# Maximum product ahead of the score product, and maximum ahead of the band, in the steps of a cross attention

## What is computed

```
Q = (query @ Wq + bq).reshape(Bsz, S, NUM_HEADS, D_K)
K = (key @ Wk + bk).reshape(Bsz, S, NUM_HEADS, D_K)
V = (value @ Wv + bv).reshape(Bsz, S, NUM_HEADS, D_K)
scores = jnp.einsum('bqhd,bkhd->bhqk', Q, K) / math.sqrt(D_K)
...
scores = scores + bias[None]
scores = jnp.where(key_padding_mask[:, None, None, :], -jnp.inf, scores)
attn = jax.nn.softmax(scores, axis=-1)
out = jnp.einsum('bhqk,bkhd->bqhd', attn, V).reshape(Bsz, S, D_MODEL)
return out @ Wo + bo
```

## Time and profile before

| | |
|---|---|
| median of 3 runs | 2393.33 us (2389.95 to 2396.13) |
| profiled execution | 2390.08 us, span 2388.2 us |
| mean granted clock of TensorE | 0.958 of full |
| busy: PE, DVE, ACT, POOL | 2129.7, 1505.1, 1178.9, 1364.8 us |
| first pass, its units | about 94 to 883 us |

### The profile page before, as it was taken

The page is one execution under the profiler, slowest core; times in us unless marked ns, Lnnn a source line. Parts: engine busy times, 40 slices in busy tenths (PEclk is TensorE's granted clock), DMA queues, the critical chain, the costliest instruction groups (busy, mean ns, idle before and its releaser), DMA issues. The chain is left out here.

```text
span 2388.2 us, 43597 instructions
## 1 busy us (share of the span) xinstructions
PE 2129.7 (89%) x12672; PEld 972.8 (41%) x12673; DVE 1505.1 (63%) x4218; ACT 1178.9 (49%) x2316; POOL 1364.8 (57%) x1452
## 2 busy tenths in 40 slices
PE   3899999999999963899999999999985787899997
PEld 1333333333333311344444444444433343455554
DVE  3788888888888843566566566565534577344443
ACT  3355555555555442355545455454445474455554
POOL 3267767677677670265656555655651565455554
PEclk7999999999999986899999999999997898999999
DMA  5413323232232203544534345253403675666665
GB/s 173 151 58 105 101 84 116 70 109 94 89 107 76 84 6 131 146 122 118 150 95 142 117 132 143 88 152 98 142 32 134 125 163 117 109 117 115 111 110 88
DMA packets 222851, 263.78 MB, mean 110 GB/s; under 512 B 39192, under 2 KB 165004, under 8 KB 222388
## 3 DMA queue, kind: packets, MB, share of 16 engines
q1 hardware_dynamic: 197612, 212.79, 29.6%
q0 software_dynamic: 22976, 48.38, 11.7%
q10 hardware_dynamic: 2072, 0.28, 0.1%
HBM read 162.12 MB, written 86.80 MB: 104 GB/s over the span
## 5 line engine op out<-in xcount | busy, mean ns | idle before, releaser
L496 ACT ACTIVATE a_pt<-a_bank 128x512 f32<-128x512 f32 x512 | 305.2, 597 | 361.1 <-DVE a_bank L603 357.7
L1382 DVE CUSTOM_DVE_ANT_0 b_bank<-b_bank,b_tri 128x256 f32<-128x256 f32 (+3 forms) x512 | 253.8, 497 | 303.0 <-PE b_bank L1519 298.2
L614 DVE CUSTOM_DVE_ANT_0 a_bank<-a_bank,a_strip 128x512 f32<-128x512 f32 x512 | 353.4, 691 | 4.9 <-PE a_bank L757 4.0
L1167 POOL TENSOR_TENSOR b_acc<-b_acc,b_pt 128x256 f32<-128x256 f32 (+2 forms) x384 | 271.3, 727 | 89.5 <-ACT b_pt L1256 72.3
L406 POOL TENSOR_TENSOR a_acc<-a_acc,a_pt 128x512 f32<-128x512 f32 x256 | 317.1, 1274 | 3.6 <-ACT a_pt L496 3.1
L603 DVE TENSOR_TENSOR a_bank<-a_bank,a_band 128x256 f32<-128x256 f32 (+1 forms) x512 | 205.9, 403 | 132.2 <-PE a_bank L744 130.9
L1256 ACT ACTIVATE b_pt<-b_bank 128x256 f32<-128x256 f32 (+2 forms) x384 | 144.0, 384 | 190.1 <-PE b_bank L1503 179.6
L744 PE MATMUL a_bank<-a_q_stack,a_k_stack 128*128 128x512 f16 x512 | 196.3, 385 | 12.2 <-ACT a_pt L496 11.8
L757 PE MATMUL a_bank<-a_k_stack,a_q_stack 97*128 97x512 f16 x512 | 196.1, 383 | 3.6 <-DVE a_low L614 3.5
L1849 POOL DMA_INDIRECT out_dram<-c_z,c_to_row x72 | 114.1, 1585 | 138.2 <-DMA out_dram<-c_z,c_to_row 101.2
L403 POOL TENSOR_TENSOR a_acc<-a_pt 128x512 f32<-128x512 f32 x128 | 160.0, 1271 | 4.3 <-ACT a_pt L496 4.3
(11 more groups left out here) (346 smaller groups left out, 5439.4 us busy)
## 6 DMA issues: line engine op xcount, KB each, us to landing
b_q_stack<-qk_rows SPq DMA_DIRECT2D x192, 128.0 KB, 2.7
a_q_stack<-qk_rows SPq DMA_DIRECT2D x96, 128.0 KB
a_k_stack<-qk_rows SPq DMA_DIRECT2D x96, 128.0 KB
b_k_stack<-qk_rows SPq DMA_DIRECT2D x96, 128.0 KB, 2.7
a_sums<-in_x SPq DMA_DIRECT2D x34, 256.0 KB, 2.9
qk_rows<-a_qk_hi SPq DMA_DIRECT2D x64, 128.0 KB, 1.7
qk_rows<-a_qk_lo SPq DMA_DIRECT2D x64, 128.0 KB, 1.8
out_dram<-a_sums SPq DMA_DIRECT2D x32, 256.0 KB, 2.0
```

Of the source, the lines that this page charges most:

```text
L496: nc.scalar.activation(pt[:, n % SLOTS, :], st_bank[n % 2][:], ACT.Exp).then_inc(exped, 1)
L614: nc.vector.tensor_tensor_reduce(out=max_bank[step % 2][:], in0=max_bank[step % 2][:], in1=strip[:, g * HG + hh, at:at + S], scale=-1.0, s ...
L1167: nc.gpsimd.tensor_tensor(sums_of, sums_of, probs(n), ALU.add).then_inc(pooled, 1)
L1382: nc.vector.tensor_tensor_reduce(out=max_bank[step % 2][:, 0:w], in0=max_bank[step % 2][:, 0:w], in1=tri[:, at:at + w], scale=-1.0, scalar ...
```

## The change

In a step, TensorE issues the maximum product first and the score product behind it, and VectorE does the reduction first and the addition behind it. All waits stay with their instructions. The diff, whole but for lines that only moved along:

```
@@ VectorE, body(kind, b, u)
                 for step in range(STEPS):
-                    n = step - L
-                    if has_unit(kind, n):
...
-                        dve.wait_ge(scored, b * UNITS + n + 1)
-                        nc.vector.tensor_tensor(st_bank[n % 2][:, c0:c1], st_bank[n % 2][:, c0:c1], band[:, h, at:at + c1 - c0],
-                                                ALU.add).then_inc(biased, 1)
                     if has_max(kind, step):
...
                                                        accum_out=low[:, g % 2, hh * NT + i:hh * NT + i + 1]).then_inc(lowered, 1)
+                    n = step - L
+                    if has_unit(kind, n):
...
+                        dve.wait_ge(scored, b * UNITS + n + 1)
+                        nc.vector.tensor_tensor(st_bank[n % 2][:, c0:c1], st_bank[n % 2][:, c0:c1], band[:, h, at:at + c1 - c0],
+                                                ALU.add).then_inc(biased, 1)
@@ TensorE, body(kind, b, u)
                 for step in range(STEPS):
+                    if has_max(kind, step):
...
+                        if kind != "first" or step >= 3 * GS + 2:
+                            pe.wait_ge(lowered, b * UNITS + step + (GS - 1))
+                        mm(max_bank[step % 2][:], q_stack[0:MASK + 1, h, i * P:(i + 1) * P], k_stack[0:MASK + 1, h, :],
+                           start=True, stop=True).then_inc(maxed, 1)
                     n = step - L
                     if has_unit(kind, n):
...
                         mm(st_bank[n % 2][:], k_stack[:, h, j * P:(j + 1) * P], q_stack[:, h, :], start=True,
                            stop=True).then_inc(scored, 1)
-                    if has_max(kind, step):
...
-                        mm(max_bank[step % 2][:], q_stack[0:MASK + 1, h, i * P:(i + 1) * P], k_stack[0:MASK + 1, h, :],
-                           start=True, stop=True).then_inc(maxed, 1)
                     fill(kind, b, step, False)
```

More of the change, by code:

```diff
@@ L617, in body @@
                                                        accum_out=low[:, g % 2, hh * NT + i:hh * NT + i + 1]).then_inc(lowered, 1)
+                    n = step - L
+                    if has_unit(kind, n):
+                        j, hh = divmod(n % GS, HG)
+                        h = n // GS % NG * HG + hh
+                        c0, c1 = max(0, j * P - BAND // 4), min(S, j * P + P + BAND // 4)
+                        at = c0 - (j * P - BAND // 4)
+                        dve.wait_ge(scored, b * UNITS + n + 1)
+                        nc.vector.tensor_tensor(st_bank[n % 2][:, c0:c1], st_bank[n % 2][:, c0:c1], band[:, h, at:at + c1 - c0],
+                                                ALU.add).then_inc(biased, 1)
                     for t, (at, _, _) in enumerate(moments_at(kind)):
@@ L731, in body @@
                 for step in range(STEPS):
+                    if has_max(kind, step):
+                        g = (step // GS + 1) % NG
+                        i, hh = divmod(step % GS, HG)
+                        h = g * HG + hh
+                        if step % GS == 0:
+                            pe.wait_ge(stacked[g], (b + (2 if g == 0 else 1)) * STK)
+                            if kind == "first":
+                                pe.wait_ge(sides_stored, 16 * 3)
+                        if kind != "first" or step >= 3 * GS + 2:
+                            pe.wait_ge(lowered, b * UNITS + step + (GS - 1))
+                        mm(max_bank[step % 2][:], q_stack[0:MASK + 1, h, i * P:(i + 1) * P], k_stack[0:MASK + 1, h, :],
+                           start=True, stop=True).then_inc(maxed, 1)
                     n = step - L
```

## The result

| | before | changed |
|---|---|---|
| median of 4 runs each, same chip | 2393.69 us (2389.95 to 2396.13) | 2424.78 us (2420.23 to 2428.61) |
| ratio | 1 | 1.0130 [1.0108, 1.0153] |
| profiled execution, span | 2390.08, 2388.2 us | 2420.23, 2418.3 us |
| first batch, from one M transpose to the next batch's | 94.66 us | 101.98 us |
| a steady batch (five of the six; the third: 101.20, 105.60) | 101.08 us | 105.26 us |

The account below looks back on a forecast made before the run. TensorE's own stream was taken to bound the first pass. Seven batches at 2.6 us plus 0.4 for the last gave 18.6 us, added to 2393.3 for 2412 us; range 2398 to 2426.

Parts of the forecast that it names:

- The mechanism: First pass: addition waits for the reduction, exponential runs 0.61 us later in VectorE's step; score product's slack shrinks by 0.39 plus 0.04.
- step 7: Steady batch: would lose 0.25 us, swallowed by the wait for a query's low half at step 8.
- (a) to (d): Steady batch, steps 12 to 14, 18 to 24, 25 to 31, and 35, 39, 47, 51: 2.6 us lost together.
- (d): Steps 35, 39, 47 and 51, no late eviction: score product's slack falls short of 0.48, 0.72 us lost.
- (a) to (c): Steps 12 to 14, 18 to 24, 25 to 31: evictions behind late exponentials delay low halves; 0.2, 1.05 and 0.66 us lost.
- Larger: Each of a batch's 16 groups of four steps loses 0.39 us: 44 us, 2437; chance 0.13.
- The clock: More short idle times bring the lower clock, one stretch per batch: 7 us on top, 2419; chance 0.05.
- No change: Slack absorbs the late exponential or evictions are ready earlier; only (d) counts: 5 us, 2398; chance 0.14.
- faster: With the maximum ahead, VectorE works through TensorE's waits at the score product: up to 12 us back, 2381; chance 0.05.

Follow-up runs that it names:

- e3: The changed kernel without the empty instruction between VectorE's wait for the maximum product and the reduction; 2420.50 us, 1.0104 of the kernel before.
- e9: The kernel before without the empty instruction ahead of the reduction; 2397.00 us, 0.9997 of the kernel before.
- e1: The kernel before with the new order on TensorE only, VectorE still adding first; 2408.17 us, 1.0042 of the kernel before.
- e4: The kernel before with one more empty instruction, between VectorE's wait for the score product and the addition; 2399.49 us, 1.0007 of the kernel before.

## Why the prediction was right, and where it was not

The time came out inside the range, and the mechanism is the one forecast; the size was 1.7 times the likeliest one.

- **What bounds the pass: right.** Only the first pass moved. It is 35.7 us longer in the profile: 7.3 for the first batch, 25.3 for the six steady ones, about 3 in the last. The other two passes took 1505.4 us before and 1499.8 after; in the profiles of this study they lie between 1500 and 1515, so that is no effect of the change.
- **The mechanism: right.** The exponential starts 1.10 us after VectorE's step does (452.39 to 453.49) and did so after 0.46 (434.20 to 434.66): 0.64 later, forecast 0.61. Losses stand at the four places named, and step 7's was in good part swallowed at steps 8 and 0. Parts (a) to (d) measured 0.4, 1.1, 0.8 and 1.4 us, and step 16 another 0.15; forecast 0.2, 1.05, 0.66 and 0.72. So the largest share of the 1.6 us a batch by which the forecast fell short is (d)'s, 0.7.
- **The step that failed** is the sentence that a step of VectorE "is as long as before and begins at the same moment, since the maximum product now stands in the score product's old slot". The slot is the same, but a reduction that was waited for starts 0.53 us behind its product, the addition 0.41 to 0.43: an empty instruction stands between wait and reduction. The slack of a score product shrank by about 0.54, not by 0.43, at every place at once: steps 35 and 51 lost 0.30 where I had 0.14 and 0.15, and step 16, which I had taken as free, began to pay. Nor is such a step always "as long as before": (d) was to be "with no late eviction", but in step 44 there is one, VectorE's step is 0.23 longer, most of it (0.19) in waiting for that eviction, and step 47 lost 0.55 where I had 0.25, with the empty instruction and, in e3 (0.51), nearly as much without. e3 measures 103.91, 2.83 over before, beside a forecast of 2.6. That the two sums are so near is partly luck: in e3, (d) is 1.06 and not 0.72, while steps 7, 8 and 0 together give 0.18 back. The 0.53 was to be had from the trace of before (90.69 and 91.24), had I looked up how long each of the two waits takes to let go.
- **The range: held by luck.** 31.1 us lies outside the 10 to 28 that had the chance of 0.63. The upper end, 2426, added 13 us for "(a) to (c) half as large again"; but these three were 7 x 1.91 = 13.4 us in all, so half of them is 6.7, and the end by its own rule would have been 2419, below the 2424.78 measured. Nor were these parts what grew most: they were larger by some 0.4 us a batch, (d) by 0.7, and the first and the last batch by 5 to 8 us together.
- **First and last batch: mis-sized.** I charged the first 2.6; it lost 5.0 to 7.7. Without output fills in steps 12 to 27 it has less to cover lateness with, part of it is the clock, and near copies of the kernel before scatter by some 3 us there without either (e9). How it divides was not tried. The last lost about 3, not 0.4; TensorE still waits there for GpSimd's sums, but these come later themselves, as they need the exponentials. That is argued from GpSimd's inputs, not shown by a run.
- **The rivals.** *Larger*, with a loss in each group: no, whole groups of four, such as steps 52 to 59, lose nothing. *The clock*: it fell in the first batch (1.7 and 3.4 us' worth), where the change is not shown to be what brings it, and not where I had put it: with 18 new waits the steady batches keep 1.00. The Trainium skill, "TensorE: Matmul & The Clock Gate", section "A second HAM failure mode: psum-queue depth-cycling", lets short idle times between groups of matmuls make the clock swing; the traces of the changed kernel agree for the thinly filled first batch at most, and not for the steady ones. *No change* and *faster*: refuted, the latter by e1 too, where the maximum ahead on TensorE alone costs 1.45 a batch.
- **What would show it.** The steady batch: 105.26, forecast 103.7. TensorE's busy time: forecast unchanged, up by 1.7 us. The score product's waits: three per batch and 1.0 us, forecast six and 1.6. The low halves at the transposes: seen. VectorE's busy time: 84.9 to 85.2 a batch, 84.7 to 84.8 before.

## What to carry to other kernels

In this kernel, between two operations of a loop, the one whose result comes back to the bounding engine soonest had to go first, and the one that is needed a group of steps later last; the wrong order cost, at each place, the delay less the slack there, and nothing where fills cover it. An operation that is made late also delays what is queued behind it on its engine; look there for the next wait. Before an instruction is moved to where its engine waits, look up how long that wait takes to let go, with whatever small instruction stands behind it. And read the list of waits of the bounding engine as a list of what to put first: here it was low halves, and moving five of them won 11 us.

## What the runs showed of the hardware

An empty instruction on VectorE costs nothing measurable behind running work (e9, 0.9997) and about 0.1 us behind a wait that stops the engine: 0.53 to 0.55 us from a product's start to the reduction with it, 0.42 to 0.43 without (e3); 0.48 to 0.50 to the addition with it (e4), 0.41 to 0.43 without. And the granted clock fell in some executions (to 0.75 over 10 us in the changed kernel) in a stretch where TensorE is busy 65 to 86% in the windows shown, with waits up to 1.5 us, though not in the two profiles of the kernel before, where it is busy 68 to 72% between 106 and 126 us; while 2.2 to 2.5 us more idle time in a batch that is 95% busy, in waits of at most 1.0 us, left it at 1.00.
